# Layer two's expert stage: all tokens through all experts, or rows sorted by expert

## The reference, cut to what matters

```python
logits = xt @ gate_w.T                                  # xt: (4096, 128)
scores = jax.nn.softmax(logits.astype(jnp.float32), axis=-1)
biased = scores + gate_b.astype(jnp.float32)
idx = jax.lax.top_k(biased, TOP_K)[1]                   # 2 of 8 experts for each token
weights = (jnp.take_along_axis(scores, idx, axis=-1) * ROUTE_SCALE).astype(x.dtype)
cw = jnp.sum(jax.nn.one_hot(idx, E, dtype=x.dtype) * weights[..., None], axis=1)
h1 = jnp.einsum('td,efd->etf', xt, w1) + b1[:, None, :]
h3 = jnp.einsum('td,efd->etf', xt, w3) + b3[:, None, :]
a = swiglu(h1 * h3)                                     # width 256 -> 128
y = jnp.einsum('etf,edf->etd', a, w2) + b2[:, None, :]
routed = jnp.einsum('te,etd->td', cw, y)
sh = swiglu((xt @ sw1.T + sb1) * (xt @ sw3.T + sb3))    # shared expert, every token
shared = sh @ sw2.T + sb2
return (routed + shared).reshape(inp_shape)
```

## Time and profile before

| | us |
|---|---|
| median of 3 runs | 1907.16 |
| lowest and highest | 1906.37, 1907.27 |
| the profiled execution | 1911.44 |
| its span, first to last instruction | 1909.6 |
| prologue and scan | 0 to about 490 |
| experts0 | 490 to 620 |
| attention, with its inputs and output | 620 to 1505 |
| experts1, norm and routing | 1505 to 1577 |
| experts1, loop over 72 steps | 1577 to 1909.6 |

### The profile page before, as it was taken

One profiled execution on the slowest core, in us unless ns is written; L12 is line 12 of the kernel. 1 busy time (PEld: TensorE's weight loads), 2 busy tenths in 40 slices (PEclk: granted clock), 3 DMA queues, 4 the chain that ended last, 5 costly groups with the idle time before them and its releaser, 6 DMA issues. The chain is left out here.

```text
span 1909.6 us, 42021 instructions
## 1 busy us (share of the span) xinstructions
PE 1586.4 (83%) x15322; PEld 1026.0 (54%) x15322; DVE 1444.9 (76%) x3721; ACT 938.4 (49%) x2029; POOL 596.7 (31%) x598
## 2 busy tenths in 40 slices
PE   1277777767469299999999999999998379999996
PEld 0177777666444245555555555555555265555553
DVE  6699999997569646666666666666666727999999
ACT  1455555554210226666666666666665123444442
POOL 3486666661113315111211211121100303333332
PEclk7688888888679589999999999999999659999998
DMA  1000000000000012111111111111100000000001
GB/s 67 0 1 1 1 1 1 1 1 0 12 1 1 17 18 40 29 27 28 32 29 26 31 30 26 30 31 28 28 20 9 20 1 2 13 8 14 7 7 45
DMA packets 100092, 32.50 MB, mean 17 GB/s; under 512 B 91186, under 2 KB 92228, under 8 KB 99780
## 3 DMA queue, kind: packets, MB, share of 16 engines
q1 hardware_dynamic: 99332, 30.07, 8.5%
q10 hardware_dynamic: 576, 0.07, 0.0%
HBM read 15.43 MB, written 2.10 MB: 9 GB/s over the span
## 5 line engine op out<-in xcount | busy, mean ns | idle before, releaser
L1135 DVE TENSOR_REDUCE ntop<-score 128x1 f32<-128x512 f32 x512 | 318.2, 684 | 253.7 <-PE score L1016 253.7
L1094 ACT ACTIVATE prob<-score,ntop 128x512 f32<-128x512 f32 x512 | 317.7, 687 | 270.8 <-DVE ntop L1135 270.8
L371 ACT ACTIVATE hist<-zp 128x168 f32<-128x168 f32 (+1 forms) x768 | 224.1, 313 | 171.3 <-DVE zp L340 170.6
L1052 PE MATMUL turned<-ident,prob 128*128 128x128 f32 x2048 | 268.5, 280 | 1.4 <-DVE probT L1078 1.4
L421 PEld LDWEIGHTS py<-hist,diagC 128*128 128x128 f32 x2048 | 262.9, 214 | 0.0
L421 PE MATMUL py<-hist,diagC 128*128 128x128 f32 x2048 | 262.7, 297 | 0.0
L1016 PE MATMUL score<-ks,qs 64*128 64x512 f32 x1024 | 257.6, 622 | 0.0
L1052 PEld LDWEIGHTS turned<-ident,prob 128*128 128x128 f32 x2048 | 219.0, 141 | 49.4 <-issue 27.4
L391 POOL TENSOR_TENSOR xb<-xc,Bm 128x1024 f32<-128x1024 f32 x128 | 244.9, 1952 | 1.3
L335 DVE TENSOR_TENSOR gp<-hist,Ap 128x168 f32<-128x168 f32 (+1 forms) x768 | 231.1, 331 | 14.7 <-POOL xb L391 14.7
L340 DVE TENSOR_TENSOR zp<-gp,xb 128x168 f32<-128x168 f32 (+1 forms) x768 | 234.7, 336 | 0.0
(11 more groups left out here) (236 smaller groups left out, 1934.0 us busy)
## 6 DMA issues: line engine op xcount, KB each, us to landing
tb<-in_table SPq DMA_DIRECT2D x64, 127.1 KB
rel_q<-q_sb SPq DMA_DIRECT2D x256, 8.0 KB
ks<-k_sb SPq DMA_DIRECT2D x32, 128.0 KB
key_q<-q_sb SPq DMA_DIRECT2D x248, 8.0 KB
w<-in_ew SPq DMA_DIRECT2D x9, 320.0 KB, 2.8
x<-in_x SPq DMA_DIRECT2D x1, 2048.0 KB, 8.8
q_sb<-cm SPq DMA_DIRECT2D x64, 32.0 KB
k_sb<-inv SPq DMA_DIRECT2D x64, 32.0 KB
```

Source lines behind the costliest of these rows:

```text
L371: nc.scalar.activation(hist[:, par, u, lo:hi], zp[j][:, 0:hi - lo], ACT.Tanh)\
L1052: last = nc.tensor.transpose(turned_ps[BANK[e]][:, j * P:(j + 1) * P], prob[G % 2][e][:, j * P:(j + 1) * P], ident[:, :])
L1094: nc.scalar.activation(prob[G % 2][e][:, :], score_ps[r][:, :], ACT.Exp, bias=ntop[:, G % 2, e:e + 1]).then_inc(prob_ready, 1)
L1135: v.tensor_reduce(ntop[:, G % 2, e:e + 1], score_ps[r][:, :], AX.X, ALU.max, negate=True)\
```

## The change

Layer two's loop is replaced. Tokens are split into two parts of 16 tiles. After the routing, DVE works out for each of the two chosen experts of a token a row number in a list that is sorted by expert, each expert's rows padded to a multiple of 256 (`SLOTS`). Counting needs prefix sums over tokens, which TensorE gives with 36 matmuls of `chosen` against a triangle and a matrix of ones. POOL scatters the rows of `h` to DRAM (`sorted_h`, one indirect DMA of 128 rows for each tile and choice, 64 in all), and gathers the experts' results back from `sorted_y` with another 64. Each part has a fixed number `RB` = 23 of list blocks of 256 rows, whatever the tokens choose; `eid` tells the expert of each.

The loop now has N = 62 steps of 256 columns: 16 of the shared expert (`NSHARED`, from `hT` directly) and 46 routed ones. For a routed step SP reads the expert's number from SBUF into a register, loads its 320 KB of weights into one of `NW` = 3 buffers, and loads 256 sorted rows; TensorE transposes them (`turn`). ACT copies the result (`take`) and SP stores it. The clips move from POOL to DVE. A gathered tile is added by DVE in `combine`. The loop is unrolled, with no hardware loop.

In both expert stages the logit matmuls of block j-1 now follow the transposes of block j. The norm's semaphores are shared between its three uses. In the scan stage SP writes zeros over both lists (2 x 2.9 MB). `acc` is seeded by the shared expert, whose down matmuls take the `b2` matmul along.

```diff
+PARTS = 2
+PT = NT // PARTS
+SLOTS = 2 * P
+RB = 2 * PT * P // SLOTS + NE1 - 1
+NROUTED = PARTS * RB
@@ Normed.tensor (follow is the logits of one block)
             last.then_inc(self.t_ready, 1)
+            if follow and j:
+                pe.wait_ge(self.hT_ready, self.all0 + j)
+                follow(j - 1)
@@ experts1, sync
+    NW, NX, NY, NGOT = 3, 4, 4, 8
+    AFTER = 3
+            def load_weights(m):
+                if m >= NW:
+                    sp.wait_ge(y_ready, NSHARED + m - NW + 1)
+                e = sp.value_load(eid[0:1, m:m + 1], min_val=0, max_val=NE1)
+                sp.dma_start(W[m % NW][:, :], d["ew1"][bass.ds(e, 1), :, :].rearrange("o p n -> p (o n)"))\
+                  .then_inc(routed_in[m % NW], 16)
+            def load_slots(m):
+                if m % RB == 0:
+                    sp.wait_ge(scattered[m // RB], 16 * 2 * PT)
+                if m >= NX:
+                    sp.wait_ge(xs_turned, m - NX + 1)
+                sp.dma_start(xs[m % NX][:, :, :], hs[m // RB][...])
+            def store(m):
+                sp.wait_ge(y_taken, NSHARED + m + 1)
+                sp.dma_start(ys[m // RB][...], ysb[m % NY][:, :, :]).then_inc(y_out[m % NY], 16)
+            load_slots(0)
+            for m in range(NROUTED):
+                if m + 1 < NROUTED:
+                    load_slots(m + 1)
+                load_weights(m)
+                if m >= AFTER:
+                    store(m - AFTER)
@@ experts1, gpsimd
+            for s in range(PARTS):
+                for k in range(s * PT, (s + 1) * PT):
+                    for r in range(2):
+                        g.indirect_dma_start(out=hs[s][:, :], out_offset=bass.IndirectOffsetOnAxis(ap=pos[:, r, k:k + 1], axis=0),
+                                             in_=norm.h[:, k, :], in_offset=None).then_inc(scattered[s], 16)
+            for s in range(PARTS):
+                for i in range(NY):
+                    pool.wait_ge(y_out[i], 16 * stores(i, (s + 1) * RB))
+                for k in range(s * PT, (s + 1) * PT):
+                    for r in range(2):
+                        g.indirect_dma_start(out=got[:, k % NGOT * 2 + r, :], out_offset=None, in_=ys[s][:, :],
+                                             in_offset=bass.IndirectOffsetOnAxis(ap=pos[:, r, k:k + 1], axis=0))
@@ experts1, vector (the loop)
+            LATE = NSHARED + RB + AFTER + 2
+            for n in range(N + 1):
+                if n < N:
+                    gates(n)
+                if n >= 1:
+                    join(n - 1)
+                if n < N:
+                    lins(n)
+                k = n - LATE
+                if 0 <= k < PT:
+                    combine(k)
@@ experts1, tensor
+            pe.wait_ge(pos_ready, 1)
+            def up(n):
+                    m = n - NSHARED
+                    w, src = W[m % NW], xT[:, m % 2, :]
+                    pe.wait_ge(routed_in[m % NW], 16 * ring(m, NW))
+            for n in range(N + 2):
+                if NSHARED <= n + 1 < N:
+                    turn(n + 1)
+                if n < N:
+                    up(n)
+                if n >= 2:
+                    down(n - 2)
```

More of the change, by code:

```diff
@@ L1272, in back, with ring, stores @@
[L1272 to L1282 removed]
+        CONSTS = 6
+        def ring(m, n):
+            return m // n + 1
+        def stores(i, m):
+            return len(range(i, m, NY))
@@ L1304, in _ @@
+            load_slots(0)
[5 more added lines that the diff above has]
+                    store(m - AFTER)
+            for m in range(NROUTED - AFTER, NROUTED):
+                store(m)
             for j in range(NBLK):
@@ L1362, in _, with bias, slots, gate @@
-            experts(act, body)
-            tanh(*back(NE1, 0, NBLK, 1))
+                A.copy(cwT[:, j * BLK:(j + 1) * BLK], pm[2 + j % 2][0:NALL, :]).then_inc(cwT_ready, 1)
+            def bias(n, c):
+                return ball[:, NE1, c:c + 1] if n < NSHARED else bsel[:, n - NSHARED, c:c + 1]
+            def slots(n):
+                m = n - NSHARED
+                act.wait_ge(xs_turned, m + 1)
+                A.copy(xT[:, m % 2, :], XT[m % 2][:, 0:SLOTS]).then_inc(xT_ready, 1)
+            def gate(n):
+                act.wait_ge(gate_ps, n + 1)
+                if n >= 2:
+                    act.wait_ge(gg_raw, n - 1)
+                A.activation(g1[:, n % 2, :], G1[:, 0:SLOTS], ACT.Identity, bias=bias(n, 0)).then_inc(first_g, 1)
@@ new lines, in take @@
+            def take(n):
+                act.wait_ge(y_ready, n + 1)
+                if n < NSHARED:
+                    dst = acc[:, n * HALVES:(n + 1) * HALVES, :]
+                else:
+                    m = n - NSHARED
+                    if m >= NY:
+                        act.wait_ge(y_out[m % NY], 16 * (m // NY))
+                    dst = ysb[m % NY][:, :, :]
+                A.copy(dst.rearrange("p o e -> p (o e)"), Y[n % 2][:, 0:SLOTS]).then_inc(y_taken, 1)
+            act.wait_ge(w_in, 16 * 4)
@@ new lines, in _ @@
+            chain(v.tensor_reduce(nblk[:, :, :].rearrange("p s e -> p (s e)"), over[:, :, :], AX.X, ALU.add))
+            for s in range(PARTS):
+                chain.add(v.tensor_tensor(bef[:, s, :, :], nblk[:, s, :].unsqueeze(1).to_broadcast([P, NE1, NE1]),
+                                          earlier[:, :, :], ALU.mult))
+            chain.wait()
+            chain(v.tensor_reduce(first[:, :, :], bef[:, :, :, :], AX.X, ALU.add))
+            chain(v.tensor_scalar(base[:, :, :], first[:, :, :], float(SLOTS), None, ALU.mult))
@@ L1441, in _, with combine @@
-            experts(dve, body)
-            join(*back(NE1, 0, NBLK, 1))
-            for j in range(NBLK - 2, NBLK):
-                add_up(*back(NE1, 0, NBLK, NBLK - j))
-                finish(j)
+            def combine(k):
+                dve.wait_ge(got_in[k % NGOT], 32 * ring(k, NGOT))
+                for r in range(2):
+                    v.scalar_tensor_tensor(acc[:, k, :], got[:, k % NGOT * 2 + r, :], wt[:, r, k:k + 1], acc[:, k, :],
+                                           ALU.mult, ALU.add).then_inc(combined, 1)
+                    dve.wait_ge(combined, 2 * k + r + 1)
@@ L1447, in _ @@
+            for k in range(min(PT, max(0, N + 1 - LATE)), NT):
+                combine(k)
+                if k % TPB == TPB - 1:
+                    finish(k // TPB)
         @block.tensor
@@ new lines, in down @@
+            def down(n):
+                w = Wsh if n < NSHARED else W[(n - NSHARED) % NW]
+                if n == 0:
+                    pe.wait_ge(shared_half, 1)
+                pe.wait_ge(a_ready, n + 1)
+                if n >= 2:
+                    pe.wait_ge(y_taken, n - 1)
+                for o in range(HALVES):
+                    cols = slice(o * P, (o + 1) * P)
+                    if n < NSHARED:
+                        k = n * HALVES + o
+                        mm(Y[n % 2][:, cols], cwT[:, k * P:(k + 1) * P], b2[:, :], start=True, stop=False)
+                    last = mm(Y[n % 2][:, cols], a[:, n % 2, cols], w[:, 4 * P:5 * P],
+                              start=(n >= NSHARED), stop=True)
+                last.then_inc(y_ready, 1)
```

505 lines of the change are left out of this document (295 added, 210 removed).

## The result

| | us |
|---|---|
| before, median of 4 runs beside it | 1907.22 (1906.37 to 1908.00) |
| changed, median of 4 runs | 2053.69 (2048.87 to 2055.75) |
| ratio | 1.0764, 95% interval 1.0750 to 1.0777 |
| span of the profiled execution | 2051.3, mean granted clock 0.839 |

The change costs 146 us.

The account below looks back on a forecast made before the run. TensorE bounds the kernel before; afterwards late weight loads bound the routed steps. 1623 us up to the late steps, plus 43 x 7.85 = 337.6, plus 54.1 gives a 2014.7 span, hence 2012 us; range 1930 to 2080.

Parts of the forecast that it names:

- The late load: Routed steps: three buffers give weights no lead, so from m = 3 on, 43 steps each take a full circle.
- The size of the circle: Each late routed step: 6.2 us at full clock, 8.4 at low; one in four at full clock gives 7.85.
- The 0.6 for the TENSOR_LOAD: Late step's circle: SP's load of the expert's number costs 0.6 us, within bounds of 0.05 and 2.8.
- A shared step: Shared expert's 16 steps: TensorE takes 2.58 us each, including 0.43 for two bias matmuls; about 2.6 a step.
- Logits: Both expert stages: logits put between transposes end 6.3 us earlier in each, 12.6 in both.
- Routing: Between logits and loop: `pos` 29.2 us after the logits' end, first `gates` at 35.5, which is +3.1.
- The zeroing: Start of the scan: zeroing 5.8 MB is costed at nothing; if not hidden, 30 us.
- The indirect transfers: POOL's scatters and gathers: 1.3 us each, bounds 0.36 and 4.05; part 0's scatters hide under the shared steps.
- The end: After the last routed step: part 1's 32 gathers, covered by nothing, and what surrounds them take 54.1 us.
- One: Rival for the routed steps: clock holds at 1.00, circle 6.2 us, time 1941; chance 0.24.
- Two: Rival: DVE holds up POOL, 2.6 us a transfer, time 2050, or 2092 with the end's gathers; chance 0.14.
- the rule of the Trainium skill: POOL's DMAs: GpSimd cannot write descriptors during DVE's two-port copy-like operations, so clips on DVE would delay scatters.

Follow-up runs that it names:

- 1: Changed kernel with five weight buffers instead of three: 1938.31 us, ratio to before 1.0151.
- 6: Changed kernel with five weight buffers and both loads (weights and rows) two steps ahead in SP's queue: 1896.69 us, ratio 0.9946.
- 12: Changed kernel with five weight buffers, both loads two steps ahead in SP's queue and the bias products first: 1810.83 us, ratio to before 0.9494.
- 8: Changed kernel without the 32 second-bias products in the shared steps, that bias left out of the result: 2105.03 us.
- 9: Changed kernel with each shared step's products reordered to bias, bias, product, product in one accumulation group: 2046.46 us.
- experiment 4: Kernel before with only the logit matmuls following each transposed block, in both layers: 1893.89 us, ratio 0.9920.
- experiment 7: Changed kernel with seven dummy products in each of the 43 late steps, where TensorE waits for weights: 2043.33 us.
- experiment 5: Changed kernel run once more with nothing changed, on another occasion: 2118.69 us.
- 2: Changed kernel with four weight buffers instead of three: 1946.24 us, ratio to before 1.0184.
- 3: Changed kernel with the expert's number loaded into SP's register ahead of the wait for y_ready: 2092.29 us.
- 10: Changed kernel with all 64 of POOL's indirect scatters replaced by plain stores issued by SP: 2051.97 us.
- 11: Changed kernel with the first half's 32 indirect scatters replaced by plain stores issued by SP: 2050.30 us.

## Why the prediction was right

It gave 2012, 1930 to 2080, slower; measured were 2053.69. The cause was the one named. Point by point:

- **The late load: right.** The wait stands in the profile after 43 times; five buffers and an earlier issue take it away (1, 6, 12), and with it, less the 7 us of the biases, 236 of the 243 us between 2053.69 and 1810.83.
- **The size of the circle: 7.85 said, 8.50 measured**, 43 x 0.65 = 28 us, the largest miss, from two terms about alike. At the low clock I had 8.4, and the 20 circles with all their work at 0.50 take 8.76; 0.25 of it is the way from the issue to the first product, 3.35 on average (141 us in 42 circles) for my 3.1. And I had a quarter of the steps at full clock, where under a tenth of the work ran at it, 19 of 198 us. The earlier trace rows had shown how long TensorE worked before the clock rose (until 128.8, as the mean of 0.70 in the last half microsecond has it, and not 128.6), and I counted the work in a circle as nearly enough. The clock did rise, but mostly as a piece of work ended. TensorE was busy 203 of 366 us, a little over the half that I gave as the most. The 0.6 for the TENSOR_LOAD, my own number and the floor that the prediction cites, was 0.27, and the 0.15 for the register work 0.24.
- **A shared step: 2.6 said, 3.39 measured.** I took the price of a bias product from eight equal products in a row, where no change of shape shows. Experiments 8 and 9 give the price of the change. The scatters still hid under these steps.
- **Logits: 6.3 a layer said, 7.0 measured** (14 in both, experiment 4).
- **Routing: right.** `pos` 29.1 after the logits for 29.2 (1562.29 less 1533.2), the first product with bias at 36.0 for 35.5.
- **The zeroing: right.** The first transposes start at 1512.08, those of experiment 4, without it, at 1511.23.
- **The indirect transfers: right**, 1.3 said, 1.26 to 1.29 measured (0.96 of POOL and 0.30 between two), landing 2.2.
- **The end: 54.1 said, 56.4 measured** (1994.9 to 2051.3), with a term that the prediction lacks. The last output has landed at 2047.0, but the span waits for POOL, whose closing DRAIN takes 7.90 us behind the gathers, to 2050.8 (rows below, ns and start). Experiment 12 has the same 7.90; the kernel before ends 0.3 us after its last output. The other terms were 2 us too long together.

```profile
L1271 POOLq DRAIN  x1: 7901/7901/7901, 2042.9 to 2042.9; - x1
L1271 SPq COMPARE_BRANCH  x1: 33/33/33, 2047.0 to 2047.0; - x1
```

By position the misses add up like this. The first `gates` came 3.0 early (1569.2 for 1572.2), 1.4 of it from the logits. From there to the end of the third routed step's first products, where the circles start, were 60.7 us for 50.8 (to 1629.9); that is what the longer shared steps cost. The circles took 365.0 for 337.6 and the end 2.3 more: together 36.6, and 2051.3 - 2014.7 is 36.6. The other 5 us between 2012 and 2053.69 lie in the step from span to median: I had taken 2.5 off the span, as the profiled execution before lay above its median, and here the median lies 2.4 above the span.

**The rivals.** One, a clock that holds at 1941, did not happen; experiment 7 shows its circle as 6.41. Two had the right time, 2050, for a wrong reason: POOL's transfers kept 1.26 to 1.29 us throughout, beside DVE's clips too. Of the rule of the Trainium skill ("SBUF — State Buffer", section "SBUF: two separate sides") the trace shows little: a clip that meets the end of a scatter ends just behind it, and 11 of the 40 clips beside scatters take 0.35 to 0.53 us instead of 0.29.

```profile
1572.44 1.01 POOL L1414 DMA_INDIRECT sorted_h<-hz,pos  x1 [0.30 <-issue]
1573.05 0.50 DVE L1581 TENSOR_SCALAR ll<-ll 128x256 f32<-128x256 f32 x1
```

The longest scatter takes 1.25, and all 64 lose some 2 us, (1.29 - 1.26) x 63. On some occasions POOL goes on while ACT and SP stand still (experiment 5). The prediction had nothing of that. It would have put 2118.69 outside the range; that the runs of the result fell on an occasion without it was luck.

**Left open.** What makes ACT and SP stand still. Shown is that it comes and goes with the occasion and not with the edit (5 against after), and that it was seen beside indirect transfers: the scatters (1 to 3, 5 to 8) and the first gathers (6, and one circle each of 3 and 7, while in 5 no two loads there are more than 9.4 us apart). The programs without such transfers, before and 4, kept their times on the same occasions (1908.69 and 1893.89), but they also keep the hardware loop in place of unrolled code, and no run separates the two. That the transfers cause it was not shown, as 10 and 11 came when it was absent. The DMA view of 1577 to 1630 tells nothing either: the scatters' queue takes 13.0% of the DMA engines in both profiles of the changed kernel, and the two queues that load instructions move 4 packets in the kernel after and 2 in experiment 5.

## What to carry to other kernels

A ring of buffers gives the lead that its release and its place in the issuing queue leave, not its size: for each load, write down which event frees the slot and which waits stand ahead of it on the queue, and count the steps from there to the use. Here three buffers gave none, four and five gave one step, and issuing the loads a step further ahead gave the rest, some 236 us in all. A mean clock over a stretch with rests says little until the stretch is cut at the work.

## What the runs showed of the hardware

- In a loop of about 5 us of work and 3.4 of rest the granted clock was 1.00 for 98 of 141 us of rest and 19 of 198 us of work (1631 to 1988 above). Seven useless products in each rest kept it at 1.00 and saved 75 us.
- Going from 9-row to 128-row weights or back cost TensorE 0.2 us each time at full clock; two equal in a row cost nothing extra (3.39 and 3.01 us a step).
- An indirect transfer of 128 rows cost POOL 0.96 us and 0.30 to the next, within 0.3 us whatever the others did. With them POOL's DRAIN at the end of the program took 7.90 us.
- On some occasions ACT and SP stood still for some 60 us beside such transfers and SP's issues took 0.70 us instead of 0.36, in the very program that showed nothing of it on others.
